# A change of layer in a local-attention stack: the next weights loaded between the last tile's v stores, and converted in two tiles instead of one

## What is computed

```python
for i in range(DEPTH):                                            # 6 layers
    x = attn_layer(shift_tokens(x), Wqkv[i], q_scale[i], k_scale[i], Wo[i]) + x
    x = ffn_layer(shift_tokens(x), ln_g[i], ln_b[i], W1[i], b1[i], W2[i], b2[i]) + x

def attn_layer(x, Wqkv, qs, ksc, Wo):
    q, k, v = jnp.split(x @ Wqkv, 3, -1)                          # 128 -> 3 * 1024, 16 heads of 64
    ...                                                           # l2norm, scale, rotary tables on q and k
    out = local_attention(q, k, v)                                # windows of 32, each sees itself and the one before
    return out @ Wo

def ffn_layer(x, g, bln, W1, b1, W2, b2):
    xn = (x - mu) / jnp.sqrt(var + 1e-05) * g + bln
    a, gate = jnp.split(xn @ W1 + b1, 2, -1)
    return a * jax.nn.gelu(gate, approximate=False) @ W2 + b2
```

## Time and profile before

| | us |
|---|---|
| median of 3 runs | 3723.23 |
| lowest and highest | 3721.95, 3728.84 |
| the profiled execution, its own time | 3732.04 |
| its span in the profile | 3730.2 |

### The profile page before, as it was taken

The page is one execution under the profiler, slowest core; times in us unless marked ns, Lnnn a source line. Parts: engine busy times, 40 slices in busy tenths (PEclk is TensorE's granted clock), DMA queues, the critical chain, the costliest instruction groups (busy, mean ns, idle before and its releaser), DMA issues.

```text
span 3730.2 us, 148973 instructions
## 1 busy us (share of the span) xinstructions
PE 3456.9 (93%) x64612; PEld 2719.9 (73%) x64612; DVE 2801.6 (75%) x4876; ACT 2369.3 (64%) x4307; POOL 2810.4 (75%) x3470
## 2 busy tenths in 40 slices
PE   4799986999989999899999899998999998999996
PEld 2565544788877888777888778887788887788774
DVE  3487566888877888778888778887788887788762
ACT  3333223677767777677777677776777776777662
POOL 1355546998878888788888788887888887888771
PEclk9798997999999999999999999999999999999998
DMA  3323212211111111111111121111111111111110
GB/s 109 101 81 91 84 32 58 49 41 38 48 44 49 40 43 43 46 44 45 41 39 45 44 51 38 44 42 47 43 46 40 43 40 46 44 43 47 38 37 23
DMA packets 126733, 183.48 MB, mean 49 GB/s; under 512 B 29824, under 2 KB 61440, under 8 KB 126080
## 3 DMA queue, kind: packets, MB, share of 16 engines
q1 hardware_dynamic: 119232, 146.15, 15.6%
q0 software_dynamic: 6848, 27.80, 2.5%
HBM read 59.01 MB, written 14.16 MB: 20 GB/s over the span
## 4 chain that ended last, share of the span: by engine, by line
PE 84%; POOL 4%; DVE 3%; issue 3%; ACT 2%; DMA 2%; SPq 0%; another core or an unknown queue 0%; ACTq 0%; POOLq 0%; DVEq 0%
PE bank L533 22%; PE bank L605 10%; PE bank L616 9%; PE bank L578 7%; PE bank L543 5%; PE bank L553 4%; PE bank L589 4%; PE bank L679 3%; PE bank L657 3%; PE bank L668 3%; PE bank L565 2%; PE bank L448 1%; PE bank L508 1%; PE bank L625 1%; PE bank L487 1%
## 5 line engine op out<-in xcount | busy, mean ns | idle before, releaser
L533 PE MATMUL bank<-wqkv,xs 128*128 128x512 f32 x3456 | 1068.6, 425 | 17.6 <-DVE m L954 13.0
L1537 POOL TENSOR_TENSOR m<-m 128x512 f32<-128x512 f32 x576 | 728.8, 1286 | 30.0 <-DVE m L954 27.2
L533 PEld LDWEIGHTS bank<-wqkv,xs 128*128 128x128 f32 x3456 | 586.8, 192 | 147.0 <-issue 57.3
L1244 ACT ACTIVATE sq<-bank 128x512 f32<-128x512 f32 x768 | 458.6, 597 | 105.5 <-PE bank L533 61.4
L954 DVE TENSOR_TENSOR m<-bank,tab 128x512 f32<-128x512 f32 x768 | 523.0, 681 | 0.7 <-POOL m L1537 0.3
L1545 POOL TENSOR_TENSOR S<-S,nw 128x1024 f32<-128x1024 f32 x192 | 383.3, 1996 | 163.7 <-DVE S L985 163.7
L965 DVE TENSOR_REDUCE ss<-sq 128x8 f32<-128x512 f32 x768 | 506.0, 676 | 0.0
L1553 POOL TENSOR_TENSOR S<-S,rs 128x512 f32<-128x512 f32 x384 | 411.1, 1091 | 64.5 <-DVE rs L999 63.3
L605 PEld LDWEIGHTS bank<-P,big 64*64 64x64 f32 x24576 | 378.3, 135 | 81.4 <-issue 73.6
L952 DVE TENSOR_TENSOR m<-bank,tab 128x512 f32<-128x512 f32 x576 | 393.0, 682 | 59.0 <-ACT sq L1244 43.7
L605 PE MATMUL bank<-P,big 64*64 64x32 f32 x24576 | 400.8, 220 | 5.0 <-issue 3.7
(11 more groups left out here) (232 smaller groups left out, 6471.1 us busy)
## 6 DMA issues: line engine op xcount, KB each, us to landing
big<-vst SPq DMA_DIRECT2D x1536, 64.0 KB, 2.0
stage<-in_wqkv SPq DMA_DIRECT2D x36, 256.0 KB, 3.0
tab<-in_tab SPq DMA_DIRECT2D x48, 128.0 KB, 2.2
xsort<-big SPq DMA_DIRECT2D x4, 960.0 KB, 8.7
big<-xsort SPq DMA_DIRECT2D x12, 256.0 KB, 6.6
ysort<-big SPq DMA_DIRECT2D x12, 256.0 KB
wo<-in_wo SPq DMA_DIRECT2D x6, 512.0 KB, 3.7
big<-in_x SPq DMA_DIRECT2D x8, 256.0 KB, 3.8
```

The costliest lines, as they stand in the source:

```text
L533: m = eng.matmul(pb[:, :], xt[a], wqkv[:, z, 512 * part:512 * part + 512], start=(n == 0), stop=(n == 2))
L1244: eng.activation(sq[:, part % 2, :], bank[part % 2][:, :], ACT.Square, scale=1.0, bias=0.0).then_inc(s["a_sq"], 1)
L1537: eng.tensor_tensor(turned(g, part), turned(g, part), m2[:, part % 2, :], ALU.add).then_inc(s["g_add"], 1)
```

## The change

Nothing is computed otherwise; instructions change places in three lists. SP issues the loads of w2 and w3 ahead of the first group of v stores of tile 31, the load of w4 between the two groups, and the load of w5 behind the second. ACT converts w2 and w3 ahead of `v_out(n, 1)`, and w4 and w5 in tile 32 behind `turned_q` of tile 31. DVE converts w2 and w3 at the end of tile 31, behind `norm_step`, and w4 and w5 in tile 32 ahead of `rotate(n, 0)`.

```diff
@@ block.sync
                     for par in range(2):
+                        if n % 32 == 31 and l + 1 < DEPTH:
+                            for j in (0, 1) if par == 0 else (2,):
+                                m = TURN[j + 2]
+                                q.wait_ge("v_w", 6 * (l + 1) + j + 1)
+                                eng.dma_start(stage[:, j % 2, :], wqkv_d[l + 1, :, 512 * m:512 * m + 512]).then_inc(s[f"d_st{j % 2}"], 16)
                         q.wait_ge("a_vst", 2 * n + par + 1)
...
                     if n % 32 == 31 and l + 1 < DEPTH:
-                        for j in range(4):
-                            m = TURN[j + 2]
-                            q.wait_ge("v_w", 6 * (l + 1) + j + 1)
-                            eng.dma_start(stage[:, j % 2, :], wqkv_d[l + 1, :, 512 * m:512 * m + 512]).then_inc(s[f"d_st{j % 2}"], 16)
+                        q.wait_ge("v_w", 6 * (l + 1) + 4)
+                        eng.dma_start(stage[:, 1, :], wqkv_d[l + 1, :, 512 * TURN[5]:512 * TURN[5] + 512]).then_inc(s["d_st1"], 16)
@@ block.vector
                 reduced(n - 1, 3)
                 largest(n - 3)
                 lessened(n - 3)
+                weights(n - 1, 4)
+                weights(n - 1, 5)
...
                 rotate(n, 2)
-                weights(n, 2)
-                weights(n, 3)
                 rotate(n, 3)
-                weights(n, 4)
-                weights(n, 5)
                 reduced(n, 2)
                 if q4 == 3:
                     norm_step(u - 2)
                     end_step(u - 5)
+                weights(n, 2)
+                weights(n, 3)
@@ block.scalar
                 turned_q(n - 1, 0)
                 turned_q(n - 1, 1)
+                weights(n - 1, 4)
+                weights(n - 1, 5)
                 square(n, 0)
...
                 out_turned(n - 4, 0)
-                v_out(n, 1)
                 weights(n, 2)
                 weights(n, 3)
-                weights(n, 4)
-                weights(n, 5)
+                v_out(n, 1)
```

## The result

The changed kernel takes 3691.75 us (3688.14 to 3692.47) against 3723.22 us: a ratio of 0.9915, 95% interval 0.9903 to 0.9928. That is 31 us; 37 was forecast. On another chip, on which the kernel before takes 3737 us, the same comparison gave 0.9920 (0.9907 to 0.9933).

What follows compares the result with a forecast made beforehand. PE bounds the kernel, busy 93% of the span, with a hole at five changes of layer. Each change: 10.9 - 3.9 + 0.7 - 0.3 = 7.4 us; five give 37, so 3723.2 - 37 = 3686 us, range 3674 to 3703.

Steps and rivals of the forecast that it cites:

- The sum for one change: At each of five changes of layer: 7.4 us won, five times 37 us.
- The old hole, 10.9: PE's second q transposes of tile 31 wait for DVE's `norm_step`; this idleness goes, 10.9 us a change.
- tile 39's distances: Tile 39, like tile 31 but without weights, shifted 140.14 us to place the new order; `norm_step` at 1058.97.
- The new hole, 3.9: PE's output projection waits for ACT's softmax copy, queued behind w5, whose load follows the v stores: 3.9 us a change.
- the bound of 5.0: Upper end of PE's new wait before the output projection, forecast between 3.6 and 5.0 us.
- 1.2 was the worst case: DVE's low half of w2 behind `norm_step`: 0.69 us beside an idle POOL, the longest 1.20.
- The clock, +0.7: Half clock behind PE's hole, taken to come two times in three: 1.4 of 2.1 us stays, 0.7 won a change.
- the prediction's 2.1 us: Extra time of the tile behind PE's hole, without waits for instructions, over five changes; taken for the clock.
- Instructions, -0.3: Two loads landing while PE works disturb its instructions: 0.3 us lost a change, bounds 0 and 1.2.
- The scale: The 37 us were taken from the median 3723.2 us, 8.8 us below the profiled execution's 3732.04.
- The rule: Skill page: two-SBUF-input DVE instructions and SBUF-reading POOL ones exclude each other wholly; the prediction held contention adds 0.5 us.
- The rival built on it (the third in the list): One POOL add, 1.5 us, stands ahead of DVE's w2: hole 4.9 us, time 3691 us; chance 0.10.

Runs made afterwards that it cites:

- the one that made it longer: The changed kernel with w5 loaded twice, the second load issued when the first has landed: ratio 0.9951 to the kernel before, scaled 3705 us.
- the matmuls in the hole: The changed kernel with 13 matmuls nobody reads ahead of a layer's first output projection: ratio 0.9903 to the kernel before, scaled 3687 us.

## Why the prediction was right

The sum for one change was 10.9 - 3.9 + 0.7 - 0.3 = 7.4 us; the tiles show 7.0. The mechanism held: the old wait went, and the new one stands where it was placed and for the cause that was named. That the sum came so close is in part luck, since the misses in its smaller terms nearly cancel. Term by term:

- **The old hole, 10.9.** Right in place and size. `norm_step` runs at 1050.02; the placing on tile 39's distances said 1049.9 on this profile's clock, which is 9.09 us ahead. w2 and w3 landed in time and `v_out` stayed hidden, as worked out.
- **The new hole, 3.9.** Right in place and cause, shown by the run that took it away by changing ACT's order and by the one that made it longer; mis-sized: 4.85 us, in one case (5.41) beyond the bound of 5.0. Three steps of the chain at the first change were each a little late: w2's low half took 1.38 us where 1.2 was the worst case (w4's issue is 0.4 us late), the four stores behind w4's issue took 2.95 us instead of 2.5, and w5's round trip 2.92 instead of 2.72. The stores vary most: 2.95, 3.34, 2.80 and 2.41 us at the first, third, fourth and fifth change, and the holes there are 4.91, 5.41, 4.96 and 4.12 us. At the second the stores took 2.41 us and w5's load, from issue to use, 3.43.
- **The clock, +0.7.** Wrong. I let it stay in one hole of three; it fell in or right behind all five of the profile, since the output projection takes 3.03 to 3.75 us behind each. In the first one it fell 2.1 us after PE's last matmul had ended; in the fifth 0.8 us after PE had begun again. At most 0.1 us a change was won: by the measure of the prediction's 2.1 us, which is the excess of tile 32 and its like without its waits, it is 2.0 us now. That measure is somewhat high as a price of the clock, which is 1.8 us by the time PE worked at half clock and 1.6 by the matmuls in the hole.
- **Instructions, -0.3.** The step that failed by its reading: the 12.9 us are `wo`'s landing, as the run with `wo` earlier shows, and say nothing of instructions. Nothing was lost to such waits either: in tile 32 and its like they come to 0.74 us in five, where they were 2.3 us before. That is 0.3 us a change won instead of 0.3 lost.
- **Not in the sum.** Tile 31 before was longer than tile 39 by 11.9 us, its hole of 10.9 and 1.0 us more; now it is longer by 0.4. The second q transposes ran at half clock behind the old hole (1.09 us for four in the earlier trace rows, 1.09 us for eight now). These 0.6 us, and the 0.6 us between 0.3 won and 0.3 lost in the line above, stand against misses of 0.95 us for the new hole and 0.6 us for the clock. That leaves 7.0 for 7.4: the agreement of the sum is better than that of its terms, and that is luck.
- **The scale.** I took the profile's 8.8 us above the median for scatter that concerns no step. That fits the 8.9 us by which its tile 1 begins later than that of after.
- **Where 34.9 us of tiles become 31.5 us of median.** Tiles 36 and 37 take 4.8 us more in the profile of after, since the output projection behind `wo`'s hole ran slow at three changes there and at one before. Whether the change does that or it falls so is not settled; all kernels with `wo` late lie between 156.7 and 165.4 there.

**The rule.** I held against the page of the Trainium skill that low halves beside POOL take 1.2 us, less than a whole POOL instruction. The profile of after has the case that decides, POOL and DVE at the fifth change:

```profile
3058.30 1.90 POOL L1548 TENSOR_TENSOR S<-S,nw 128x1024 f32<-128x1024 f32 x1
```
```profile
3058.43 2.31 DVE L938 TENSOR_TENSOR wqkv<-stage,wqkv 128x512 fp32r<-128x512 f32 x1 [1.94 <-ACT wqkv L1240]
```

DVE's instruction began 0.13 us into POOL's, which ends at 3060.20, and ended at 3060.74, 0.54 us behind it. It is not alone: of the 30 low halves in this profile 19 began while a POOL instruction of over 1 us was under way, 0.14 to 2.06 us after its start, and all 19 ended 0.55 us behind that instruction's end. So DVE's did nothing while POOL's ran. The Trainium skill, "SBUF — State Buffer", Who interferes with whom, has it so, an exclusive hold for the whole instruction, and the row agrees. The 1.2 us of before were the same lock met half-way: there too the low half ends 0.55 us behind POOL's instruction. The rival built on it (the third in the list) had the mechanism right and its price too high: w2 came in the middle of an add, so 0.7 us of waiting and not 1.5. Its figures, a hole of 4.9 us and 3691 us, are nearer to the measured 4.85 and 3691.75 than mine, but not for its reason: w2's low half gives 0.4 of the 1.0 us that the first hole is longer than forecast, the stores and w5's landing the rest.

## What to carry to other kernels

When a row names the instruction that PE waits for, walk back through the lists of all engines in the path: here the named instruction stood behind a conversion, that behind a load, that behind stores, and freeing only the first gave 1.7 us of 10.9. A conversion of the next weights belongs behind everything on its engine that a bank is waiting for, and just ahead of its own first use; and a load that only has to land belongs ahead of stores that nobody waits for. A wait that the profile ends with "issue" may be a wait for a transfer: compare its end with issue time plus landing time before it is called anything else.

## What had not been expected of the hardware

- The granted clock fell behind rests of 2.03 us (the run with matmuls in the hole) and 2.55 us, while rests of 2.9 and 3.3 us in the kernel before had left it alone. It did not always fall during the rest: at the fifth change of after it fell 0.8 us after PE had begun again, and the row of that microsecond has PE busy throughout. Which rests it falls behind was not predictable from their length.

```profile
3060.00:3061.00 1.00, 1.00 (x8) 0.66 0.09 16
```

- A DVE instruction with two inputs in SBUF took 2.31 us instead of 0.69 beside one POOL instruction of 1.90 us; all 19 that met a POOL instruction of over 1 us in the profile of after ended 0.55 us behind it.
- The issue of the same four 64 KB stores, right behind the same load, took SP 2.41 to 3.34 us at the five changes of one execution. What makes the difference is open.
